# A top-2 expert layer on 256-slot tiles, with weights held in one place and gate and up computed transposed

## What is computed

```python
xn = layernorm(x)                                  # x: (8, 1024, 256), so 8192 tokens
s = ssm(xn)                                        # h_t = A h_(t-1) + (xn B_w^T + B_b); s = h C_w^T + C_b
logits = xn @ Wr + br                              # 8 experts
routing_weights, expert_indices = top_k(logits, 2); routing_weights = softmax(routing_weights)
gate = xn @ W1[e]; up = xn @ W3[e]                 # 256 -> 512
y = (silu(gate) * up) @ W2[e]                      # 512 -> 256
out = x + s * silu(sum over the two experts of weight * y)
```

## Time and profile before

| | us |
|---|---|
| median of 3 runs | 928.48 (927.62 to 929.33) |
| the profiled execution | 927.39 |
| its span, first to last instruction | 925.7 |
| PE busy | 859.3 (93%) |
| POOL / DVE / ACT busy | 427.0 / 474.1 / 385.9 |

### The profile page before, as it was taken

How to read it: one execution, slowest core, us unless ns; L and a number is a source line. 1 busy time by engine, 2 the same in 40 slices (tenths; PEclk the granted TensorE clock), 3 DMA queues, 4 the chain that set the end, 5 groups by cost and what they waited for, 6 DMA issues and landing times.

```text
span 925.7 us, 22168 instructions
## 1 busy us (share of the span) xinstructions
PE 859.3 (93%) x4860; PEld 701.9 (76%) x4861; DVE 474.1 (51%) x1072; ACT 385.9 (42%) x820; POOL 427.0 (46%) x692
## 2 busy tenths in 40 slices
PE   4899994999999989999999999999999999998796
PEld 3444442888878878888888888888888888886685
DVE  6848995755565633333333433333433333332997
ACT  4754673433343423333433433343444333332442
POOL 3312603665666665545465654445555554541000
PEclk9999997999999989999999999999999999999899
DMA  8942002311131131111131221111131111112997
GB/s 252 327 160 69 0 0 92 102 52 56 52 107 57 49 113 57 51 57 53 54 108 62 98 70 52 56 55 52 50 119 47 57 57 57 51 44 89 363 384 255
DMA packets 65402, 89.94 MB, mean 97 GB/s; under 512 B 7262, under 2 KB 52835, under 8 KB 65380
## 3 DMA queue, kind: packets, MB, share of 16 engines
q1 hardware_dynamic: 51092, 54.80, 17.6%
q0 software_dynamic: 13056, 34.62, 11.6%
q10 hardware_dynamic: 1232, 0.28, 0.2%
HBM read 56.12 MB, written 34.60 MB: 98 GB/s over the span
## 4 chain that ended last, share of the span: by engine, by line
PE 74%; issue 9%; DVE 5%; DMA 5%; POOL 3%; POOLq 1%; ACT 1%; ACTq 1%; DVEq 0%; SPq 0%
PE bank L1066 36%; PE bank L1070 18%; PE bank L1165 5%; PE bank L1119 5%; PE bank L1006 3%; PE bank L1088 3%; DMA x_sb<-L_attn_x 2%; DMA xg<-xn_rows,gi_ring 1%; DMA yy<-y_rows 1%; POOL W_sb L384 1%; PE bank L968 1%; PE bank L1161 1%; DVE h_sb L775 1%; PE bank L1046 1%; DVE stats L652 1%
## 5 line engine op out<-in xcount | busy, mean ns | idle before, releaser
L1066 PE MATMUL bank<-W_sb,xh 128*128 x1088 | 310.0, 407 | 2.4 <-DVE xl L811 2.3
L838 DVE TENSOR_TENSOR hl<-bank,hh 128x512 fp32r<-128x512 f32 x136 | 94.0, 691 | 283.4 <-ACT hh L600 266.2
L406 POOL DMA_INDIRECT y_rows<-y_sb,si_ring x136 | 142.6, 1049 | 187.9 <-ACT y_sb L610 115.7
L1066 PEld LDWEIGHTS bank<-W_sb,xh 128*128 128x128 f32 x1088 | 187.2, 191 | 27.0 <-issue 3.5
L398 POOL DMA_INDIRECT xg<-xn_rows,gi_ring x136 | 149.3, 1098 | 113.0 <-POOL gi_ring L396 98.9
L1066 PE MATMUL bank<-W_sb,hh 128*128 x1088 | 164.1, 293 | 9.4 <-ACT hh L600 9.4
L1070 PE MATMUL bank<-W_sb,xl 128*128 x544 | 169.8, 393 | 0.0
L600 ACT ACTIVATE hh<-bank 128x512 fp32r<-128x512 f32 x136 | 81.1, 596 | 187.7 <-PE bank L1119 172.1
L1066 PEld LDWEIGHTS bank<-W_sb,hh 128*128 128x128 f32 x1088 | 139.4, 190 | 11.5 <-issue 11.1
L1070 PEld LDWEIGHTS bank<-W_sb,xl 128*128 128x128 f32 x544 | 102.7, 189 | 24.1
L610 ACT ACTIVATE y_sb<-bank 128x256 f32<-128x256 f32 x136 | 52.3, 384 | 145.1 <-PE bank L1070 136.4
(11 more groups left out here) (172 smaller groups left out, 826.4 us busy)
## 6 DMA issues: line engine op xcount, KB each, us to landing
yy<-y_rows SPq DMA_DIRECT2D x32, 512.0 KB, 7.9
raw<-L_ffn_W SPq DMA_DIRECT2D x24, 512.0 KB
x_sb<-L_attn_x SPq DMA_DIRECT2D x16, 512.0 KB, 4.9
xn_rows<-scratch SPq DMA_DIRECT2D x16, 512.0 KB, 3.9
out<-x_sb SPq DMA_DIRECT2D x16, 512.0 KB, 7.6
xg<-xn_rows,gi_ring POOLq DMA_INDIRECT x136
y_rows<-y_sb,si_ring POOLq DMA_INDIRECT x136
h_sb<-L_attn_B_w ACTq DMA_DIRECT2D x1, 256.0 KB, 4.2
```

The lines of the kernel that those rows point to most:

```text
L406: eng.indirect_dma_start(out=y_rows, out_offset=bass.IndirectOffsetOnAxis(ap=si_ring[:, r:r + 1], axis=0), in_=y_sb[:, r, :], in_offset=No ...
L838: eng.tensor_tensor(hl[:, :], ps_hT[:, :], hh[:, :].bitcast(f32), ALU.subtract).then_inc(hl_ready, 1)
L1066: eng.matmul(o, a_high[:, k * P:(k + 1) * P], W(part, k), start=k == 0 and part == 0, stop=False)
```

## The change

- Tiles have 256 slots: `EXP_TILES = 2 * T // TW + E - 1` is 71, and two columns of `gather_idx` and `scatter_idx` belong to each (142 in all instead of 136).
- Gate and up are computed transposed: blocks of 128 x 128 weights are stationary and 256 columns of `xh` or `xl` move. The result lies in four banks in the layout that the product with W2 wants, so the transposes of h are gone. `hbuf`, now 128 x 1024 for a tile and two deep, is split to `hh` and `hl` from SBUF instead of from PSUM.
- Weights have one place, at fixed addresses. The next expert's W1, W3 and W2 are split part by part when PE has done with the old part: W1 after gate and W3 after up of the last tile of the old expert, W2 after its down. ACT rounds, DVE subtracts; POOL does none of it.
- POOL reads its indices where they lie, without a copy; its list is unrolled. `tile_woff` is gone, and PE reads no table.
- PE's order in step i is gate(i+1), up(i+1), transposes of x(i+2), down(i). y is evicted one step later (`keep_y(i - 1)`), from one bank, and `y_sb` has two places of 256 rows.

The core of the diff:

```diff
-SLOT_TILES = 2 * TILES + E
+TW = 2 * P
+EXP_TILES = 2 * T // TW + E - 1
+SLOT_TILES = EXP_TILES * TW // P
...
-            def split_low(e, w):
-
-                for n in range(2):
-                    wait_apart(eng, w_high, e * 2 + n + 1)
...
-            def gather(i, r):
-                eng.tensor_copy(gi_ring[:, r:r + 1], gather_idx[:, bass.ds(i, 1)]).then_inc(gi_ready, 1)
-                wait_apart(eng, gi_ready, i + 1)
...
+            def gather(i):
+                for t in range(2):
+                    eng.indirect_dma_start(out=xg[:, i % XG_RING, t, :], out_offset=None, in_=xn_rows,
+                                           in_offset=bass.IndirectOffsetOnAxis(ap=gather_idx[:, 2 * i + t:2 * i + t + 1], axis=0))\
+                       .then_inc(xg_loaded[i % XG_RING], 16)
...
+            def high_next(i, n, first):
+
                 with eng.If(first > 0):
+                    e = eng.value_load(tile_expert[0:1, bass.ds(i, 1)], min_val=1, max_val=E - 1)
+                    eng.wait_ge(raw_loaded[n], e * 16 + 16)
+                    high(n)
...
+            def next_x(i):
+
+                first = is_first(i)
+                high_next(i, 0, first)
+                x_high(i)
+                high_next(i, 1, first)
...
+            def expert_step(i, r, stored=None, y=True, gate=True, xT=True):
+
+                if y:
+                    eng.wait_ge(tile_done, i)
+                    high_next(i, 2, is_first(i))
+                for n in range(2):
+                    eng.wait_ge(h_ready, 2 * i + (n + 1))
+                    eng.activation(hh[:, n * 512:(n + 1) * 512], hbuf[:, r, n * 512:(n + 1) * 512], ACT.Copy).then_inc(hh_ready, 1)
+                if gate:
+                    silu(i + 1, 1 - r, 0)
+                else:
                     keep_C()
+                if y:
+                    keep_y(i - 1, 1 - r, stored)
                 if gate:
+                    silu(i + 1, 1 - r, 1)
                 if xT:
+                    next_x(i + 2)
...
+            def low_next(i, n, first):
+
+                with eng.If(first > 0):
+                    e = eng.value_load(tile_expert[0:1, bass.ds(i, 1)], min_val=1, max_val=E - 1)
+                    eng.wait_ge(w_high[n], e + 1)
+                    low(n)
...
+            def expert_step(i, r, w2=True, gate=True, xT=True):
+
+                if w2:
+                    low_next(i, 2, is_first(i))
+                for n in range(2):
+                    cols = slice(n * 512, (n + 1) * 512)
+                    eng.wait_ge(hh_ready, 2 * i + (n + 1))
+                    eng.tensor_tensor(hl[:, cols], hbuf[:, r, cols], hh[:, cols].bitcast(f32), ALU.subtract).then_inc(hl_ready, 1)
...
+            def product(o, w_at, done):
+
+                for m in range(KI):
+                    part = o[m // 2][:, m % 2 * TW:(m % 2 + 1) * TW]
+                    for k in range(KD):
+                        at = w_at + k * I + m * P
+                        high, low = W_sb[:, at:at + P], W_sb[:, LO_AT + at:LO_AT + at + P]
+                        x_h, x_l = xh[:, k * TW:(k + 1) * TW], xl[:, k * TW:(k + 1) * TW]
+                        eng.matmul(part, high, x_h, start=k == 0, stop=False)
+                        eng.matmul(part, low, x_h, start=False, stop=False)
+                        last = eng.matmul(part, high, x_l, start=False, stop=k == KD - 1)
...
+            def up(i, first=False):
+                if not first:
+                    eng.wait_ge(h_ready, 2 * i)
+                    eng.wait_ge(hl_ready, 2 * i - 1)
+                product(ps_up, W3_AT, up_psum)
+
+            def down(i, first=False):
+                eng.wait_ge(hl_ready, 2 * i + 2)
+                if not first:
+                    eng.wait_ge(y_ready, i)
...
-            for i in range(2):
-                expert_step(i, i, 16, first=i == 0, reused=False)
-            with loop(eng, 2, SLOT_TILES - 2, XG_RING) as i0:
+            with loop(eng, 1, EXP_TILES - 2, XG_RING) as i0:
                 for n in range(XG_RING):
-                    expert_step(i0 + n, (n + 2) % XG_RING, i0 * 4 + 24)
...
+                    i = i0 + n
+                    gate(i + 1)
+                    up(i + 1)
+                    transpose_x((n + 3) % XG_RING, i0 * 8 - 8 + (32 if n == 0 else 64))
+                    down(i)
```

More of the change, by code:

```diff
@@ new lines, in _ @@
+            x_high(0)
+            for n in range(2):
+                silu(0, 0, n)
+            next_x(1)
+            expert_step(0, 0, y=False)
+            for i in range(1, 3):
+                expert_step(i, i % 2)
+            with loop(eng, 3, EXP_TILES - 2, 2) as i0:
+                for n in range(2):
+                    expert_step(i0 + n, (n + 1) % 2, i0 * 16 - 16)
+            last = EXP_TILES - 1
+            expert_step(last - 1, 1, 32 * (last // 2 - 1), xT=False)
+            expert_step(last, 0, 32 * (last // 2 - 1), gate=False, xT=False)
@@ L852, in _ @@
+            for n in range(2):
+                eng.wait_ge(w_high[n], 1)
+                low(n)
+            x_low(0)
+            eng.wait_ge(w_high[2], 1)
+            low(2)
+            for n in range(2):
+                mul_up(0, 0, n)
+            next_x(1)
             eng.wait_ge(A_ready, 1)
@@ L1074, in _ @@
[L1074 to L1085 removed]
+            eng.matmul(ps_val[:, 0:SLOT_TILES], zero_bf[:, 0:P], zero_bf[:, :], start=False, stop=True).then_inc(table_psum, 1)
@@ new lines, in gate @@
+            def gate(i, first=False):
+                if not first:
+                    eng.wait_ge(silu_ready, 2 * i)
+                eng.wait_ge(xl_ready, i + 1)
+                product(ps_gate, 0, gate_psum)
+            def up(i, first=False):
[5 more added lines that the diff above has]
+                eng.wait_ge(hl_ready, 2 * i + 2)
+                if not first:
+                    eng.wait_ge(y_ready, i)
+                for t in range(2):
+                    o = ps_y[:, t * D:(t + 1) * D]
+                    for k in range(KI):
+                        at = W2_AT + k * D
+                        high, low = W_sb[:, at:at + D], W_sb[:, LO_AT + at:LO_AT + at + D]
+                        h_h, h_l = (h[:, k * TW + t * P:k * TW + (t + 1) * P] for h in (hh, hl))
+                        eng.matmul(o, h_h, high, start=k == 0, stop=False)
+                        eng.matmul(o, h_h, low, start=False, stop=False)
+                        last = eng.matmul(o, h_l, high, start=False, stop=k == KI - 1)
+                last.then_inc(tile_done, 1)
@@ L1154, in _ @@
+            gate(EXP_TILES - 1)
+            up(EXP_TILES - 1)
+            down(EXP_TILES - 2)
+            transpose_C()
+            down(EXP_TILES - 1)
             eng.wait_ge(scan_done, 4 * BATCH)
```

361 lines of the change are left out of this document (118 added, 243 removed).

## The result

The changed kernel took 942.79 us (median of 4 runs, 940.33 to 943.08) beside 928.11 for the kernel before on the same chip (927.62 to 929.33): a ratio of 1.015, 95% interval 1.013 to 1.017. It is slower by 1.5%. The forecast was 917.7 with a range of 904 to 933, so the sign was wrong and the time lies outside the range.

What follows compares the result with a forecast made beforehand. PE, busy 93% of the span, was taken as the bound. The stage falling from 686.6 to 673.4 gains 13.2, ahead and behind lose 2.4: 927.4 becomes 916.6, and 1.1 for the median gives 917.7 us, range 904 to 933.

Steps and rivals of the forecast that it cites:

- the sum of the steady tile's waits: Usual tile: hl ready at g + 2.67, up's weight load due at g + 2.76, so hidden by 0.1 us; g is gate's start.
- cost nothing now and bring nothing when gone: POOL's index copies: with four indirect DMAs at about 1 us each leaving POOL half idle, removing them changes nothing.
- Rival (b): Every tile: the thin cover fails and up waits 0.15 to 0.25 in some 60 tiles, 9 to 15 us more; chance 0.15.
- the pace of 0.120: PE's gate and up: each matmul of 256 columns takes 0.120 us, read from the old down group's last four.
- up's stall at a change: W2's split at each of seven expert changes: up can load at g + 4.83, due 2.76, a stall of 2.07 us.
- All changes: Seven expert changes: 2.15 ahead of up and 0.8 ahead of gate each, plus 0.9 for scans; 21.5 us, bounds 10 to 30.
- its two chains: Expert change: W2's look-ups, rounding, subtraction and hl until up loads; W1's look-ups, subtraction and xl until gate loads.
- The end: Stage's end: down(last) waits for both halves of hl(last), able to load at 3.35 and due at 0.43; 2.9 us.
- The start: Stage's start: gate and up run at the low clock, about 2.0 us more, and gate(1) waits 1.75 for xl(1).
- Rival (a): Expert changes: the new stalls drop the clock, 7 x 2.4 = 17 us more, 934.5; chance 0.10.
- granted clock 1.00 after both: Expert changes: PE's clock stays full after the gaps behind gate (about 2.1 us) and ahead of gate (about 0.7).
- Ahead and behind: Outside the expert stage: wider one-hot tables 0.7, start 0, wider last y and scatters 1.7; 2.4 us later, within 1 and 5.

Runs made afterwards that it cites:

- one pause: Changed kernel, with POOL copying one column of 128 integers and waiting for it between the two scatters and the two gathers; 910.98 us, ratio 0.981.
- index copies back: Changed kernel, with POOL again copying each index column and waiting for it before each indirect DMA, and waiting for the row buffer; 912.16 us, ratio 0.983.
- without splits: Changed kernel without loads and splits of the weights of experts 1 to 7 and their conditional blocks; all tiles use expert 0; 906.97 us, not the whole work.
- both edits: Changed kernel, with POOL's gathers issued after gate(i+2)'s first half and ACT reading `tile_first` before its wait for `down`; 919.26 us, ratio 0.991.
- two buffers: Changed kernel, with two buffers each for hh and hl, made before the end of down(i-1), and the look-up ahead of ACT's wait; 894.96 us, ratio 0.9645.
- gathers early: Changed kernel, with POOL issuing tile i+4's two gathers after the first half of gate(i+2), not behind the scatters of tile i-1; 911.43 us, ratio 0.982.

## Why the prediction was wrong

**The step that failed** is the sum of the steady tile's waits. It took from the earlier trace rows that the end of `down` is seen at g + 0.20 and found a cover of 0.1. The row was right for the kernel before, where an index copy keeps each of POOL's DMAs apart from the last. The same text said of these copies that they "cost nothing now and bring nothing when gone". They did bring something: four indirect DMAs 1.3 apart in each tile, and behind them a message up to 1.2 us late. They also left a stall at each change of expert long enough for the lower clock to follow four times. With one pause put back the stage is 671.1, so the late message costs 29.9 us of the 701.0: about 25 are waits of up, in usual tiles and at changes, and about 5.5 the lower clock, which doesn't come in the kernel with one pause. Without it the forecast (673.4) would have held to 2.3 and the time (917.7 against 911.0) within its range. Rival (b) had the right place, a gap before up in most tiles, but the wrong size (0.15 to 0.25, not 0.5) and reason (look-up or rounding).

**Right:** the tile at 9.07 for 9.05, and the pace of 0.120. 71 tiles are 644.0. The place of the stalls at changes, too.

**Sizes.** In the prediction's terms (from when PE's weight load was due) up's stall at a change was put at 2.07. It is 1.81 on average without late messages (one pause: 1.76 to 1.87) and 2.62 in the changed kernel; PE's idle gaps in the lists are shorter, since a matmul's record lasts 0.28 at a pace of 0.12. Most of the difference to 1.81 is the hand-over from DVE to PE: 0.24 was read from a start, and 0.05 pass here (371.61 + 0.69 to 372.35). With 0.05 the cover of the usual tile is an estimated 0.3, not 0.1. All changes were forecast at 21.5. In the changed kernel they lose 18.2 ahead of up and 4.5 ahead of gate (0.5 to 0.8 each, 0.8 forecast), 22.7 in all before the lower clock is counted; with one pause it is 12.5 and 4.8. So the forecast came near by two errors that cancel, a chain read too long and a message that it didn't have. (The terms of its two chains add up to 4.86 and 9.72, not to 4.83 and 9.65, which changes little.)

**The end** took 3.7 where 2.9 were forecast, and for another reason. The prediction let the last `down` wait for hl. In the rows above hl is done at 851.98, and `down` starts at 853.47, behind the eviction of the previous y (until 853.32), which stands on ACT behind its work on C. Then the clock was at 0.50 from 854.0 to 857.4, which the sum doesn't have either. **The start:** the low clock lasted from 156.8 to 161.0, as forecast, and gate(0) and gate(1) waited 1.5 and 1.6 (1.75 forecast for the second alone).

**Rival (a)** came true in part. It had the lower clock behind each change for 17 us; it came behind four of seven, for 5.5. In these rows the length of the gap alone doesn't decide: 1.80 us was followed by it, 2.67 was not. In the kernels where the gaps ahead of up were at most 1.6 us it never came at a change. The sign "granted clock 1.00 after both" thus failed in the changed kernel, and held in the kernels without a late message. The Trainium skill (TensorE: Matmul & The Clock Gate, HAM oscillation) says that idle gaps above a certain length re-throttle the array, and the length it names is above all seven of these; the trace differs, with four of them followed by a granted clock of 0.50, and the measurement decides.

**Ahead and behind** were forecast 2.4 slower and came 1.6 faster. The cause of neither part was looked for. With the index copies back gate begins at 157.41 instead of 156.89, but with one pause, which has no copy ahead of the first gate, at 157.47, so the removed copy isn't shown to be a part of it.

## What to carry to other kernels

When a stage's wait is covered by a tenth of a microsecond, the question isn't whether each piece has a row but what the change does to the pieces that it seems not to touch; here work removed from an idle engine closed up its DMAs. Where a buffer's reuse puts a long way between two engines' groups, a second buffer that takes the wait off that way is worth more than shortening it (895 us against 908). A stall that grows by a microsecond can also bring the lower clock with it. An oddly late wait with all its parties ready is settled cheaply by a probe: let a second, idle engine wait for the same message.

## What the runs showed of the hardware

TensorE's message to other engines that a group of matmuls is done came up to 1.82 us late when POOL had issued three or four indirect DMAs about 1.3 us apart, and never later than 0.04 in the four kernels that, behind the first gathers, kept to at most two in a row (964 waits). One wait at the start of the stage without splits, behind the ninth DMA of a series, ended 2.5 us late. In the changed kernel the late message comes at the median 1.8 us behind the start of the fourth DMA (1.0 to 1.9), in the kernel with both edits 0.3 to 1.8. In the tile shown first it came at 370.06 for a gather issued at 368.23. The DMA engines' busy share for the window 366 to 371 in 40 slices of 0.125 (tenths) shows three bursts behind the end of an earlier one; the last begins in the slice at 370.25, just behind the message.

```profile
DMA  9600000005992000000009925300000000984620
```

PE went on with its next matmuls meanwhile, and ScalarE and VectorE saw the message at the same moment. Which part holds it back between them wasn't tried; that a pause of one copy is enough was. Behind the third DMA it also matters when the message is due: with two buffers it was due within 0.10 us of that DMA's start and never late (0 of 53), with both edits and with gathers early the late ones were due 0.8 to 1.3 behind it. But with both edits many that were due at 0.90 were in time, and why is open.

The granted clock fell to 0.50 for 3.4 us soon after four of seven idle gaps of 1.80 to 2.67 us in the changed kernel, and after none of the gaps up to 1.6 us at changes in the kernel with one pause.
